# Turning a softmax tile for its second matmul: 32x32 blocks on VectorE and 2,048 transfers inside SBUF in place of 1,024 transposes on TensorE

## Chip, cores and metric

The kernel runs on one core of one Trainium2 chip. The metric is the device time of one execution in microseconds. All tensors are float32; most matmuls are made of three (below).

## What is computed

Sixteen images of 32x32 pixels with 128 channels go through two layers. The first: a depthwise 3x3 convolution with three filters per channel, two 1x1 layers with a GELU between them and a residual, then attention of each pixel over its 3x3 neighbours. The second, which the change touches, is a group norm and full attention over the 1,024 pixels of an image:

```python
xn = group_norm(x, gamma, beta)
n = H * W
xf = xn.reshape(B, n, C)
q = xf @ Wq + bq
k = xf @ Wk + bk
v = xf @ Wv + bv
attn = jnp.einsum('bnc,bmc->bnm', q, k) * scale
attn = jax.nn.softmax(attn, axis=-1)
out = jnp.einsum('bnm,bmc->bnc', attn, v)
out = out @ Wp + bp
return xn + out.reshape(B, H, W, C)
```

## The kernel before

Each engine has its program written out as calls, in an order fixed by hand-written lists: `fill_program`, then `turn_program(it)` for `it` = 1 to 12, then `drain_program`. In turn `it`, image `a = it` is in its last attention, `b = it + 1` in its local attention and group norm, `c = it + 2` in its convolution and `d = it + 3` is loaded. Engines meet through semaphores only (`Count.after(n, e)` names event `e` of image `n`). Four PSUM banks `work` are shared out by a table (`BANK_PLAN` for a turn, `FILL_PLAN` and `DRAIN_PLAN` for the ends).

A float32 product is made of three matmuls with operands split in a high part (rounded to `F32R`) and a low part (the rest): `mm3` at L468 to L470. So whoever makes an operand makes two tiles, and the low part waits for the high one.

The last attention of image `n` goes through eight tiles `t` of 128 queries:

- `scores(n, t)`, TensorE: 6 matmuls into `ps_s`, 128 queries by 1,024 keys.
- `row_max`, VectorE (L1869), then `exp`, ScalarE (L1048), from `ps_s` to the SBUF tile `e`, one tile for all `t`.
- `probs_t`, TensorE (L622): eight 128x128 transposes turn `e` so that keys lie on partitions; the result is in `ps_t`.
- `et_hi_tile`, ScalarE (L1058), copies `ps_t` to the high part; `et_lo_tile`, VectorE (L1875), subtracts to the low part. `et_hi` and `et_lo` hold four tiles each; a slot is free again when the value step of its tile pair has run.
- `values(n, j)`, TensorE: 24 matmuls for the tiles 2j and 2j+1; `a_part` (ScalarE), `attended` (TensorE) and `output` (VectorE, L1887) follow, and SyncE's `store`.

SyncE issues four x_in loads an image (`load_x`, L409; 32 partitions each) and two stores (L424). GpSimd makes the low parts of the other operands (`minus`, L1439) and the residual (`residual`, L1493 and L1496); the Winograd transform's `d` and part of `t_f` are its too. VectorE's `combine` and `combine_own` (L1737, L1744) read two operands in SBUF.

Of the kernel before, what the change touches and what calls it, by code (L numbers as in the profile page):

```python
# [31 lines left out]
F32 = mybir.dt.float32  # L32
F32R = mybir.dt.float32r
# [24 lines left out]
class Count:  # L58
# [5 lines left out]
    def after(self, n, e):  # L64
# [14 lines left out]
]  # L79
FILL_PLAN = [  # L80
    ("conv", 0, 0, 3), ("conv", 1, 0, 0), ("conv", 2, 0, 3), ("conv", 3, 0, 1), ("conv", 4, 0, 2),
    ("conv", 5, 0, 0), ("conv", 0, 1, 3), ("conv", 1, 1, 1), ("conv", 2, 1, 2), ("conv", 3, 1, 0),
# [16 lines left out]
    ("as", 0, 14, 0), ("conv", 0, 15, 1), ("as", 1, 14, 2), ("conv", 1, 15, 3), ("as", 2, 14, 2),  # L99
    ("conv", 2, 15, 0), ("at", 0, 14, 0), ("as", 3, 14, 3), ("conv", 3, 15, 2), ("conv", 4, 15, 2),  # L100
# [12 lines left out]
]  # L113

STAGE_OF = dict(xt=0, conv=1, up2=1, q=1, k=1, v=1, av=2, at=2, gn=2, qq=2, kk=2, vv=2, pv=3, pj=3, s0=3, s1=3)
STAGE_OF["as"] = 2
BANK_OF = {(u, x): bank for u, x, bank in BANK_PLAN}
FILL_BANK_OF = {(u, x, n): bank for u, x, n, bank in FILL_PLAN}
DRAIN_BANK_OF = {(u, x, n): bank for u, x, n, bank in DRAIN_PLAN}
USES = FILL_PLAN + [(u, x, it + 3 - STAGE_OF[u], bank) for it in range(1, B - 3) for u, x, bank in BANK_PLAN  # L120
                    if it + 3 - STAGE_OF[u] < B] + DRAIN_PLAN

# [13 lines left out]
def bank_number(user, x, n):  # L136

    at = n - 3 + STAGE_OF[user] if isinstance(n, int) else 1
    return FILL_BANK_OF[user, x, n] if at < 1 else DRAIN_BANK_OF[user, x, n] if at >= B - 3 else BANK_OF[user, x]


def previous_user(user, x, n):

    m = n if isinstance(n, int) else 5 + 3 - STAGE_OF[user]
    bank = bank_number(user, x, m)
    before = USES[:USES.index((user, x, m, bank))]
    found = [(u, y, k) for u, y, k, b in before if b == bank]
    if not found:
        return user, -1, 0
    u, y, k = found[-1]  # L150
    return u, y, k if isinstance(n, int) else n + (k - m)


def conv_seq_kernel(nc, ins, out):
    ctx = ExitStack()
    with ctx:
# [13 lines left out]
        def placed(name, shape, offset, dt=F32):  # L170
# [71 lines left out]
        e = sb("e", [128, PIX])  # L242
        et_at = region("et_mem", 2 * TILES * HALF)
        et_hi, et_lo = (placed(f"et_{p}", [128, TILES, HALF], et_at + 4 * TILES * HALF * k, F32R)
                        for k, p in enumerate(("hi", "lo")))
        wc_f = placed("wc_f", [128, NT, 3, D], et_at)
# [22 lines left out]
        def score_tile(n, t):  # L269

            return work_all[:, 0:PIX] if is_last(n) and t % 2 else ps_s
# [8 lines left out]
            s=8, t=8).items()}  # L280
# [23 lines left out]
        max1_ready, e_ready, et_hi_ready, et_lo_ready = (  # L304
            count("max1_ready", 8), count("e_ready", 8), count("et_hi_ready", 8), count("et_lo_ready", 8))
# [18 lines left out]
                        vv=vv_lo_ready, pv=a_ready, pj=o_ready, s0=e_ready, s1=e_ready)  # L324
# [78 lines left out]
        def _(sp):  # L403
# [21 lines left out]

            def load_x(n):
# [4 lines left out]
            def fill_program():  # L431
# [3 lines left out]
                store(0, 0)  # L435
                load_x(4)
                store(0, 1)

            def turn_program(it):
                a, d = it, it + 3  # L440
                store(a, 0)
                if has_next(d + 1):
                    load_x(d + 1)
                store(a, 1)

            def drain_program():
                store(B - 3, 0)
                store(B - 3, 1)
                store(B - 2, 0)
                store(B - 2, 1)  # L450
# [1801 lines left out]
```

## Time and profile before

| | us |
|---|---|
| median of 3 runs (1060.2 to 1060.88) | 1060.43 |
| profiled execution, its own time | 1062.82 |
| its span, first to last instruction | 1060.8 |
| TensorE busy | 1021.0 |
| VectorE busy | 791.3 |
| ScalarE busy | 723.6 |
| GpSimd busy | 394.7 |
| mean granted TensorE clock | 0.993 |

The span is what the trace covers; the profiled execution's own time has what lies around it. Busy times are unions of an engine's instructions, and a busy TensorE can still be one whose matmuls overlap; what a step costs there is read from the start of one step to the start of the next. L numbers are lines of the kernel before.

### The profile page before, as it was taken

To read this page: it belongs to the slowest core of one execution; us is meant where nothing else is said; L and a number is where in the kernel's file an instruction comes from. 1 tells how busy PE (TensorE), PEld (TensorE's weight loads), DVE (VectorE), ACT (ScalarE), POOL (GpSimd) and SP (SyncE) were. 2 spreads that over 40 slices of the span, in tenths; PEclk is the share of its full clock that TensorE was granted. 3 is DMA by queue.
4 is the path that set the end of the run, shared out by engine and by line. 5 is a ranking of instruction groups with operands and counts; after the bars stand their busy time and mean duration, and the time that the engine had idled before them with its cause. 6 is when DMAs were issued, how large, how long until landed. Compare 5 with 4: busy or idle time off the path is not lost.

```text
span 1060.8 us, 21242 instructions
## 1 busy us (share of the span) xinstructions
PE 1021.0 (96%) x7060; PEld 939.6 (89%) x7060; DVE 791.3 (75%) x1628; ACT 723.6 (68%) x1377; POOL 394.7 (37%) x365
## 2 busy tenths in 40 slices
PE   5978999999999999999999999999999999999897
PEld 5857989999998999999899999989999898998776
DVE  6957779777877877788687777868777786777674
ACT  2566767767677776767767776776767677677463
POOL 4635252352515235251523525153351515232031
PEclk9989999999999999999999999999999999999999
DMA  5101010010201001010100101010020100000000
GB/s 91 22 1 21 1 31 11 11 32 1 40 0 30 10 10 30 0 36 4 30 10 0 40 0 30 10 30 10 0 40 0 30 10 10 11 2 11 11 21 21
DMA packets 85493, 18.64 MB, mean 18 GB/s; under 512 B 67536, under 2 KB 85328, under 8 KB 85456
## 3 DMA queue, kind: packets, MB, share of 16 engines
q1 hardware_dynamic: 84608, 17.77, 8.6%
q10 hardware_dynamic: 848, 0.39, 0.2%
q8 instruction: 22, 0.36, 0.2%
q14 instruction: 15, 0.12, 0.0%
HBM read 9.76 MB, written 8.39 MB: 17 GB/s over the span
## 4 chain that ended last, share of the span: by engine, by line
PE 89%; DVE 4%; issue 3%; ACT 2%; POOL 2%; DMA 0%; ACTq 0%; DVEq 0%; POOLq 0%
PE work L468 16%; PE work L470 15%; PE work L469 15%; PE ps_t L622 10%; PE ps_s L468 5%; PE ps_s L470 5%; PE ps_s L469 5%; PE work L540 4%; PE work L561 4%; PE work L596 2%; PE work L527 2%; PE work L549 1%; PE work L586 1%; POOL g_lo L1439 1%; DVE et_lo L1875 1%
## 5 line engine op out<-in xcount | busy, mean ns | idle before, releaser
L1869 DVE TENSOR_REDUCE nm<-ps_s 128x1 f32<-128x1024 f32 x124 | 151.5, 1222 | 78.8 <-PE ps_s L470 75.9
L1439 POOL TENSOR_TENSOR g_lo<-u,g_hi 128x512 fp32r<-128x512 f32 x60 | 78.3, 1306 | 351.0 <-ACT g_hi L969 351.0
L1058 ACT ACTIVATE et_hi<-ps_t 128x1024 fp32r<-128x1024 f32 x128 | 131.2, 1025 | 99.1 <-PE ps_t L622 99.0
L468 PE MATMUL work<-t_lo,wc_hi 128*128 128x256 f32 x576 | 170.3, 296 | 5.9 <-DVE wc_lo L1688 4.4
L1875 DVE TENSOR_TENSOR et_lo<-ps_t,et_hi 128x1024 fp32r<-128x1024 f32 x128 | 156.1, 1219 | 22.6 <-ACT et_hi L1058 21.0
L470 PE MATMUL work<-t_hi,wc_hi 128*128 128x256 f32 x576 | 162.7, 283 | 0.0
L469 PE MATMUL work<-t_hi,wc_lo 128*128 128x256 f32 x576 | 162.1, 281 | 0.0
L1048 ACT ACTIVATE e<-ps_s,nm 128x1024 f32<-128x1024 f32 x124 | 138.2, 1114 | 25.2 <-DVE nm L1869 23.4
L468 PE MATMUL work<-et_lo,vv_hi 128*128 128x256 f32 x512 | 148.6, 290 | 4.6 <-DVE r_tok L1887 3.8
L470 PE MATMUL work<-et_hi,vv_hi 128*128 128x256 f32 x512 | 145.0, 283 | 0.0
L469 PE MATMUL work<-et_hi,vv_lo 128*128 128x256 f32 x512 | 144.7, 283 | 0.0
L622 PE MATMUL ps_t<-const,e 128*128 128x128 f32 x1024 | 133.0, 273 | 4.1 <-DVE et_lo L1875 4.0
L622 PEld LDWEIGHTS ps_t<-const,e 128*128 128x128 f32 x1024 | 117.8, 141 | 18.9 <-ACT e L1048 4.8
L468 PEld LDWEIGHTS work<-t_lo,wc_hi 128*128 128x128 f32 x576 | 109.3, 190 | 6.8 <-issue 4.8
L469 PEld LDWEIGHTS work<-t_hi,wc_lo 128*128 128x128 f32 x576 | 109.6, 190 | 0.1
L470 PEld LDWEIGHTS work<-t_hi,wc_hi 128*128 128x128 f32 x576 | 109.1, 189 | 0.0
L468 PE MATMUL ps_s<-kk_lo,qq_hi 128*128 128x512 f32 x248 | 106.4, 429 | 0.7 <-ACT e L1048 0.7
L468 PEld LDWEIGHTS work<-et_lo,vv_hi 128*128 128x128 f32 x512 | 97.3, 190 | 10.8 <-issue 9.7
L470 PE MATMUL ps_s<-kk_hi,qq_hi 128*128 128x512 f32 x248 | 98.0, 395 | 0.0
L469 PEld LDWEIGHTS work<-et_hi,vv_lo 128*128 128x128 f32 x512 | 97.1, 190 | 0.7
L469 PE MATMUL ps_s<-kk_hi,qq_lo 128*128 128x512 f32 x248 | 97.7, 394 | 0.0
L470 PEld LDWEIGHTS work<-et_hi,vv_hi 128*128 128x128 f32 x512 | 97.1, 190 | 0.0
(182 smaller groups left out, 2352.1 us busy)
## 6 DMA issues: line engine op xcount, KB each, us to landing
x_in<-in_x SPq DMA_DIRECT2D x64, 128.0 KB, 3.4
out<-r_tok SPq DMA_DIRECT2D x32, 256.0 KB, 2.3
w_up_t<-in_L_conv_w_up SPq DMA_DIRECT2D x1, 384.0 KB, 4.2
y<-in_L_conv_w_qkv SPq DMA_DIRECT2D x1, 192.0 KB, 4.9
const<-in_const ACTq DMA_DIRECT2D x1, 166.0 KB, 5.8
y<-in_L_conv_w_up ACTq DMA_DIRECT2D x1, 128.0 KB, 5.3
const<-in_const ACTq DMA_DIRECT2D x1, 64.0 KB, 3.6
bv_row<-in_L_conv_b_qkv SPq DMA_DIRECT2D x1, 64.0 KB, 2.9
```

The source lines that it names most:

```text
L468: te.matmul(dst, wh, xl, start=first, stop=False)
L469: te.matmul(dst, wl, xh, start=False, stop=False)
L470: return te.matmul(dst, wh, xh, start=False, stop=last)
L527: mm = te.matmul(bank("v", half, n)[:, t * 128:(t + 1) * 128], h[:, pix], wv0[:, :], start=True, stop=True)
L540: mm = te.matmul(dst, q_c[:, t * 128:(t + 1) * 128], kp[:, 4 * t:4 * t + 6, :].rearrange("p r w -> p (r w)"), start=True, stop=True)
L561: te.matmul(dst[:, u * 128 - before:(u + 1) * 128 + behind], v_pix[:, t, :], pt[half][:, at - before:at + 128 + behind], start=(u == 0), s ...
L622: mm = te.transpose(ps_t[:, kt * 128:(kt + 1) * 128], e[:, kt * 128:(kt + 1) * 128], ident)
L1048: act.activation(e[:, :], score_tile(n, t)[:, :], ACT.Exp, bias=nm1[:, t:t + 1], accum_out=sum1[:, t:t + 1]) \
L1058: act.activation(et_hi[:, :, (t % 4) * 128:(t % 4 + 1) * 128], ps_t[:, :].rearrange("p (k c) -> p k c", k=TILES), ACT.Copy) \
L1439: return pool.tensor_tensor(dst, full, hi, ALU.subtract)
L1869: dve.tensor_reduce(nm1[:, t:t + 1], score_tile(n, t)[:, :], AX.X, ALU.max, negate=True) \
L1875: dve.tensor_tensor(et_lo[:, :, cols_], ps_t[:, :].rearrange("p (k c) -> p k c", k=TILES), et_hi[:, :, cols_].bitcast(F32), ALU.subtract). ...
```

## The change

`probs_t`, its semaphore and its 1,024 transposes go. In their place stand `turn_e` on VectorE, which transposes `e` in 32x32 blocks, and `move` on SyncE, which carries each group of 32 partitions to where it belongs, in sixteen transfers a tile. `e` and the turned tile `turned` are double. `et_f`, the full turned tile, lies in the memory of `et_lo`. `et_hi_tile` reads `et_f` in SBUF; `et_lo_tile` moves to GpSimd and works in place. The columns of `et_hi` and `et_lo` are laid out in blocks, so that `values` reads 256 columns in runs of 32. `scores` writes to `ps_s` and `ps_t` in turn, for every image.

```diff
-        e = sb("e", [128, PIX])
+        e_both = sb("e", [128, 2, PIX])
+        turned_both = sb("turned", [128, 2, 4, TILES, 32])
...
-            return work_all[:, 0:PIX] if is_last(n) and t % 2 else ps_s
+            return ps_t if t % 2 else ps_s
...
+            def move(n, t):
+                ready, read = e_turned.after(n, t), pe["pv"].after(n, t // 2 - 2)
...
+                if t % 2 == 0:
+                    sp.wait_ge(*read)
...
+                sp.wait_ge(*ready)
+                for i in range(4):
+                    for s in range(4):
+                        sp.dma_start(et_f[32 * i:32 * (i + 1), t % 4, s].rearrange("r k q -> r (k q)"),
+                                     turned_both[32 * s:32 * (s + 1), t % 2, i].rearrange("r k q -> r (k q)")) \
+                          .then_inc(e_fetched[t % 4].handle, 16)
...
-                if not is_last(n) or t == 0:
-                    te.wait_ge(*e_ready.after(n, t - 1))
...
+                te.wait_ge(*e_ready.after(n, t - 2))
...
-            def probs_t(n, t):
...
-                for kt in range(TILES):
-                    mm = te.transpose(ps_t[:, kt * 128:(kt + 1) * 128], e[:, kt * 128:(kt + 1) * 128], ident)
...
-                             (et_hi[:, kt, cols_], et_lo[:, kt, cols_]), kt == 0, kt == TILES - 1)
+                             [x[:, two, :, kt, :].rearrange("p t s q -> p (t s) q") for x in (et_hi, et_lo)],
+                             kt == 0, kt == TILES - 1)
...
-                act.wait_ge(*pe["t"].after(n, t - 1))
+                act.wait_ge(*e_turned.after(n, t - 2))
...
+            def turn_e(n, t):
+                dve.wait_ge(*e_ready.after(n, t))
+                dve.wait_ge(*e_fetched[(t - 2) % 4].after(n, (t - 2) // 4))
+                dve.transpose(turned_both[:, t % 2].rearrange("p i k q -> p k i q"),
+                              e_both[:, t % 2].rearrange("p (k i q) -> p k i q", k=TILES, i=4)).then_inc(e_turned.handle, 1)
```

All call lists and bank tables are new. `BANK_PLAN` has a fourth number, how many images ahead of the turn a step works; a turn now ends with the third value step of its image, and the fourth is in the next turn:

```diff
-    ("as", 0, 0), ("conv", 0, 2), ("as", 1, 3), ("conv", 1, 1), ("at", 0, 0), ("conv", 2, 3), ("as", 2, 2),
+    ("at", 0, 1, 3), ("as", 2, 1, 1), ("vv", 1, 0, 2), ("pv", 3, -1, 1), ("conv", 0, 2, 3), ("as", 3, 1, 0),
```

On SyncE, the rest of a turn in the loop, before, after its first store (L423 to L456 are register work and the branch back):

```order
L427 ISA
L409 ISA
L409 DMA x_in<-in_x 32x32x32
L409 ISA
L409 DMA x_in<-in_x 32x32x32
L409 ISA
L409 DMA x_in<-in_x 32x32x32
L409 ISA
L409 DMA x_in<-in_x 32x32x32
L423 REGISTER_ALU
L424 ISA
L424 DMA out<-r_tok 128x4x128
```

And now the first half of that loop's body (L441 is `move`, L426 `store`):

```order
L441 DMA et_f<-turned 32x256 x16
L432 REGISTER_ALU
L441 DMA et_f<-turned 32x256 x16
L432 ISA
L441 DMA et_f<-turned 32x256 x16
L432 REGISTER_ALU
L441 DMA et_f<-turned 32x256 x16
L425 ISA
L426 ISA
L426 DMA out<-r_tok 128x4x128
L432 ISA
L441 DMA et_f<-turned 32x256 x16
```

Eight moves of sixteen transfers stand in a turn's queue, with a store after the fourth and the four loads and a store between the sixth and the seventh.

On GpSimd, the start of a turn in the loop, before (L1493 and L1496 are the residual, L1439 low parts):

```order
L1493 TENSOR_TENSOR r_tok<-vv_hi,vv_lo 128x512
L1496 TENSOR_TENSOR r_tok<-r_tok,bp_row 128x512
L1465 ISA
L1439 TENSOR_TENSOR g_lo<-u,g_hi 128x512
L1465 REGISTER_ALU
L1439 TENSOR_TENSOR g_lo<-u,g_hi 128x512
```

And now (L1461 is `minus`, L1467 and L1477 the transform):

```order
L1461 TENSOR_TENSOR et_lo<-et_f,et_hi 128x1024
L1508 REGISTER_ALU
L1461 TENSOR_TENSOR et_lo<-et_f,et_hi 128x1024
L1465 ISA
L1467 TENSOR_TENSOR d_53<-xp 128x256 x4
L1474 REGISTER_ALU
L1475 ISA
L1477 TENSOR_TENSOR t_f<-d_54 128x8x32
```

Eight low parts of 1,024 columns a turn are now on GpSimd, between its other work.

## Rows read from the trace of the kernel before

**Rows 1.** Windows: busy us of each engine (instructions), granted clock, DMA share, GB/s.
```profile
core 0: us, PE busy (x) PEld busy (x) DVE busy (x) ACT busy (x) POOL busy (x), PEclk, DMA share, GB/s
395.60:457.90 62.30, 62.26 (x438) 57.72 (x438) 47.47 (x101) 44.81 (x85) 24.05 (x22) 1.00 0.09 17
956.00:1005.00 49.00, 44.17 (x284) 39.49 (x282) 32.90 (x72) 30.74 (x64) 5.79 (x5) 0.97 0.04 12
```

**Rows 2.** Timeline of TensorE, start and length in us; turn 1 and a later turn.
```profile
204.71 1.03 PE L622 MATMUL ps_t<-const,e 128*128 128x128 f32 x8
205.58 0.61 PE L527 MATMUL work<-wv,h 128*128 128x128 f32 x4
...
466.63 0.28 PE L468 MATMUL work<-et_lo,vv_hi 128*128 128x256 f32 x1
...
469.51 1.05 PE L527 MATMUL work<-wv,h 128*128 128x128 f32 x8
470.40 1.06 PE L596 MATMUL work<-wv,a_c 128*128 128x128 f32 x8
...
472.17 1.04 PE L622 MATMUL ps_t<-const,e 128*128 128x128 f32 x8
472.96 0.48 PE L468 MATMUL ps_s<-kk_lo,qq_hi 128*128 128x512 f32 x1
...
474.44 0.85 PE L540 MATMUL work<-kp,q_c 128*128 128x204 f32 x4
474.98 0.42 PE L468 MATMUL work<-t_lo,wc_hi 128*128 128x256 f32 x1
```

**Rows 3.** Timeline of SyncE's queue, start and length of an issue in us.
```profile
7.74 0.43 SPq L405 DMA_DIRECT2D bv_row<-in_L_conv_b_qkv  x1
...
10.12 0.43 SPq L405 DMA_DIRECT2D r_tok<-in_L_conv_Wp  x1
12.87 0.33 SPq L409 DMA_DIRECT2D x_in<-in_x  x1
```

**Rows 4.** Tiles x_in and r_tok: ns min/median/max of an issue; two timelines of one burst.
```profile
L409 SPq DMA_DIRECT2D x_in<-in_x x64: 311/434/2404, 1.2 to 837.1; - x64
...
L424 SPq DMA_DIRECT2D out<-r_tok x32: 372/412/417, 139.9 to 1058.1; - x32
...
461.44 0.35 SPq L409 DMA_DIRECT2D x_in<-in_x  x1
...
461.44 2.72 SPq L409 DMA_DIRECT2D x_in<-in_x  x4
```

**Rows 5.** DMA issues: count, KB each, median us from issue to landing.
```profile
out<-r_tok SPq DMA_DIRECT2D x32, 256.0 KB, 2.3
```

**Rows 6.** Lines by form: busy us, mean ns of one, idle before and its releasers.
```profile
L1875 DVE TENSOR_TENSOR et_lo<-ps_t,et_hi 128x1024 fp32r<-128x1024 f32 x128 | 156.1, 1219 | 22.6 <-ACT et_hi L1058 21.0
...
L1058 ACT ACTIVATE et_hi<-ps_t 128x1024 fp32r<-128x1024 f32 x128 | 131.2, 1025 | 99.1 <-PE ps_t L622 99.0
...
L1439 POOL TENSOR_TENSOR g_lo<-u,g_hi 128x512 fp32r<-128x512 f32 x60 | 78.3, 1306 | 351.0 <-ACT g_hi L969 351.0
...
L1887 DVE SCALAR_TENSOR_TENSOR r_tok<-work,rec,r_tok 128x128 f32<-128x128 f32 x128 | 36.1, 344 | 6.1 <-PE work L596 5.0
...
L1065 ACT ACTIVATE a_c<-work 128x256 f32<-128x256 f32 x64 | 24.5, 382 | 22.9 <-PE work L470 22.9
...
L1616 DVE STREAM_TRANSPOSE xp<-x_in 128x512 f32<-128x512 f32 x30 | 19.7, 691 | 0.4 <-DMA x_in<-in_x 0.3
...
L1455 POOL TENSOR_TENSOR t_f<-d 128x256 f32<-128x256 f32 x15 | 11.1, 740 | 35.5 <-DVE d L1623 35.5
```

**Rows 7.** Tile u (ns min/median/max), and timelines of VectorE and GpSimd in the fill.
```profile
L1737 DVE SCALAR_TENSOR_TENSOR u<-u x30: 671/681/1234, 37.0 to 928.9; 128x512 f32<-128x512 f32 x30
...
52.58 3.48 DVE L1744 SCALAR_TENSOR_TENSOR u_one<-u_one 128x512 f32<-128x512 f32 x2
...
52.09 1.73 POOL L1439 TENSOR_TENSOR g_lo<-u,g_hi 128x512 fp32r<-128x512 f32 x1 [1.25 <-ACT g_hi L969]
```

More of the change, by code:

```diff
@@ L424, in store @@
                 sp.dma_start(out_view[:, bass.ds(n * TILES + 4 * k, 4), :], r_tok[:, :, :]).then_inc(stored.handle, 16)
+            def move(n, t):
+                ready, read = e_turned.after(n, t), pe["pv"].after(n, t // 2 - 2)
+                if not isinstance(n, int):
+                    ready, read = ((handle, sp.to_reg(value)) for handle, value in (ready, read))
+                if t % 2 == 0:
+                    sp.wait_ge(*read)
+                if is_first(n) and t == 0:
+                    sp.wait_ge(*g_lo_ready.after(1, 3))
+                    sp.wait_ge(*h_ready.after(1, 1))
+                sp.wait_ge(*ready)
[4 more added lines that the diff above has]
+                          .then_inc(e_fetched[t % 4].handle, 16)
             def load_x(n):
@@ L434, in fill_program @@
                 load_x(3)
-                store(0, 0)
-                load_x(4)
-                store(0, 1)
+                move(0, 0)
+                move(0, 1)
+                move(0, 2)
+                move(0, 3)
             def turn_program(it):
[L440 to L444, printed above, removed]
-            def drain_program():
+                z, a, d = it - 1, it, it + 3
+                move(z, 4)
+                move(z, 5)
+                move(z, 6)
+                move(z, 7)
+                store(z, 0)
+                move(a, 0)
+                move(a, 1)
+                load_x(d)
+                store(z, 1)
+                move(a, 2)
+                move(a, 3)
+            def drain_program():
+                move(B - 4, 4)
+                move(B - 4, 5)
+                move(B - 4, 6)
+                move(B - 4, 7)
+                store(B - 4, 0)
+                move(B - 3, 0)
+                move(B - 3, 1)
+                store(B - 4, 1)
+                move(B - 3, 2)
+                move(B - 3, 3)
+                move(B - 3, 4)
+                move(B - 3, 5)
+                move(B - 3, 6)
+                move(B - 3, 7)
                 store(B - 3, 0)
+                move(B - 2, 0)
+                move(B - 2, 1)
+                move(B - 2, 2)
+                move(B - 2, 3)
                 store(B - 3, 1)
+                move(B - 2, 4)
+                move(B - 2, 5)
+                move(B - 2, 6)
+                move(B - 2, 7)
                 store(B - 2, 0)
+                move(B - 1, 0)
+                move(B - 1, 1)
+                move(B - 1, 2)
+                move(B - 1, 3)
+                move(B - 1, 4)
+                move(B - 1, 5)
                 store(B - 2, 1)
+                move(B - 1, 6)
+                move(B - 1, 7)
                 store(B - 1, 0)
                 store(B - 1, 1)
-            fill_program()
-            turn_program(1)
-            with sp.Fori(2, B - 4) as it:
-                turn_program(it)
-            turn_program(B - 4)
-            drain_program()
+            run(sp, fill_program, turn_program, drain_program)
             sp.wait_ge(*stored.after(B - 1, 1))
@@ L755, in fill_program @@
-                q(2, 1)
-                values(0, 3)
-                scores(1, 0)
-                attended(0, 1)
-                v(2, 1)
+                scores(0, 6)
+                scores(0, 7)
+                up2(2, 1)
+                k(2, 0)
+                group_moments(1)
+                q(2, 0)
+                values(0, 1)
+                v(2, 0)
+                kk(1, 0)
+                kk(1, 1)
+                qq(1, 0)
+                v(2, 1)
+                qq(1, 1)
+                k(2, 1)
@@ L987, in k_half @@
                 act.wait_ge(*pe["k"].after(n, k))
+                act.wait_ge(*pe["as"].after(n - 1, 3))
                 if is_first(n):
@@ L1198, in fill_program @@
[L1198 removed]
+                local_scale(1, 2)
+                pt_pair(1, 1)
+                pt_pair(1, 2)
+                local_exp(1, 3)
                 et_hi_tile(0, 1)
[L1200 to L1209 removed]
@@ new lines, in turn_program @@
+                t_hi_part(c, 1)
+                take(c, 0, 1)
+                t_hi_part(c, 2)
+                local_exp(b, 3)
+                et_hi_tile(a, 0)
+                pt_pair(b, 1)
+                local_scale(b, 2)
+                local_scale(b, 3)
+                take(c, 2, 3)
+                et_hi_tile(a, 1)
+                exp(a, 4)
+                pt_pair(b, 2)
+                pt_pair(b, 3)
+                gelu(c, 0)
+                gelu(c, 1)
+                g_hi_part(c, 0)
@@ new lines, in turn_program @@
+                local_scale(c, 0)
+                exp(b, 1)
+                exp(b, 2)
+                et_hi_tile(a, 7)
+                local_exp(c, 1)
+                local_exp(c, 2)
+                t_hi_part(d, 0)
+            def drain_program():
+                pt_pair(B - 2, 0)
+                t_hi_part(B - 1, 1)
+                local_scale(B - 2, 1)
+                exp(B - 3, 3)
+                a_part(B - 4, 3)
+                vv_hi_half(B - 3, 0)
+                exp(B - 3, 4)
+                take(B - 1, 0, 1)
+                vv_hi_half(B - 3, 1)
+                et_hi_tile(B - 3, 0)
+                t_hi_part(B - 1, 2)
+                pt_pair(B - 2, 1)
@@ new lines, in turn_program @@
+                turn_e(a, 7)
+                x_turn(d, 1)
+                local_mask_max(c, 0)
+                local_mask_max(c, 1)
+                qq_lo_half(b, 1)
+                row_max(b, 0)
+                row_max(b, 1)
+                transform_even(d)
+                local_rec(c, 0)
+                turn_e(b, 0)
+                row_max(b, 2)
+                local_mask_max(c, 2)
+                row_max(b, 3)
+                turn_e(b, 1)
+            def drain_program():
+                transform_two(B - 1)
+                halo_turn(B - 2, 0)
+                local_rec(B - 2, 1)
+                row_max(B - 3, 4)
+                vv_lo_half(B - 3, 0)
+                turn_e(B - 3, 2)
+                output(B - 4, 1)
+                transform_ends(B - 1)
+                halo_turn(B - 2, 1)
+                local_mask_max(B - 2, 3)
+                local_rec(B - 2, 2)
+                vv_lo_half(B - 3, 1)
+                sum_and_difference(B - 1, 1, 2, 1)
+                turn_e(B - 3, 3)
+                row_max(B - 3, 5)
```

1101 lines of the change are left out of this document (505 added, 596 removed), and 58 rows, old and new, of tables (BANK_PLAN, DRAIN_PLAN, FILL_PLAN).

## Prediction, made before the change was run

> **What bounds the kernel now.** I read the busy time by stretches first, then neighbouring instructions in one turn of the loop, then the two engines that get the new work. In a steady turn TensorE is busy 62.26 of 62.30 us, beside 47.47 on VectorE, 44.81 on ScalarE and 24.05 on GpSimd [rows 1]. So a turn is bound by TensorE's own work and by no wait. What one step costs there is the distance from its first matmul to the first of the next step: eight transposes of e start at 472.17 and the next step at 472.96, 0.79 us; those at 204.71 are followed at 205.58, 0.87 us [rows 2]. A value step of 24 matmuls runs from 466.63 to 469.51, 2.88 us [rows 2]. The lengths printed per matmul overlap and can't be summed. SyncE has 4 loads and 2 stores a turn and is idle for the rest.
>
> **The change, part by part.** (a) *TensorE loses 1,024 transposes.* Eight groups a turn at 0.79 to 0.87 us, 0.85 taken, are 6.8 us. A turn of 62.3 becomes 55.5 if nothing else ends later. In the twelve turns (image 1 to 12 as `a`) that is 82 us.
>
> (b) *SyncE gets 16 transfers a tile, 2,048 in all*, each of 32 partitions by 1 KB, issued one after another. Call the time from one issue to the next P. No such transfer is in the trace. Six loads of 128 partitions with one run each, issued back to back, start at 7.74 to 10.12: 0.43 us each and 0.475 apart, so some 0.04 lie between two issues [rows 3]. An x_in load has 32 partitions, as the new transfers have; the first of a burst took 0.33 and 0.35, the shortest of all 0.311 [rows 3, 4]. Four in a burst took 2.72 [rows 4], but each stands behind a load of 1,024 short rows, which the new transfers don't have. Bounds for P are thus 0.353 (0.311 + 0.042) and 0.475. Both ends of the new transfers lie in SBUF, so less is possible too, and a queue that costs nothing is the outer bound. I take **P = 0.39** (0.35 + 0.04): in partitions the x_in row is the nearest. A turn's queue time is 128 P, the four loads at 2.7 us and two stores at 0.41 [rows 4], with 1.4 us for register instructions and gaps (an estimate: the burst of 2.72 has four issues of at least 0.35, and part of the rest is registers): 128 P + 4.9 = 54.8 us. That is 0.7 below TensorE's 55.5. Two queues so near each other, coupled by two e buffers, two turned buffers and four et slots, will not both run without gaps; I add 1.0. **A turn is 56.5 us.**
>
> (c) *What stands behind a move.* `move(n,t)` waits for the turned tile and, at even t, for the value step that frees two slots; SyncE's loads and stores queue behind it. From the last issue of a pair to its freed slots: landing 2.3 [rows 5], the high part 1.03 [rows 6], the low part 2.4 (below), value step 2.88, together 8.6 us. With 32 P = 12.5 for the pair's own issues that is 21.1 us, and the ring of four slots gives the time of two pairs, 28. Some 7 us are left for queueing, so the slots alone do not bound.
>
> (d) *VectorE*: the low part, 1,219 ns x128, goes; a transpose of 128x1024 comes. One of 128x512 took 691 ns [rows 6], so 1.38 at most; another instruction of 1,024 columns took the 1.22. 1.25 taken, 0.2 us more a turn. Cover: 47.7 of 56.5. (e) *ScalarE* reads SBUF where it read PSUM; 1,025 ns [rows 6] kept; 10% more would be 0.8 us a turn, under a cover of 11. (f) *GpSimd* takes the low part: 512 columns took 1,306 and 256 took 740 [rows 6], so 1,024 take 2.4 us, 19 a turn: 43.3 of 56.5, covered. With that cover gone the slots would be freed late, and SyncE would wait. (g) Scores alternate between two PSUM tiles; that removes waits that cost nothing now.
>
> (h) *The ends.* Before, turn 1 begins on TensorE at 204.7 [rows 2]. The new fill has no transposes (-6.8); a value step (2.88), half a projection and half of v's transposes (0.45 each, by eight such matmuls from 469.51 to 470.40) leave it, two scores (1.48 each, 472.96 to 474.44) and two local scores (0.54 each, to 474.98) enter [rows 2]: it ends at 198. The old drain, from 204.7 + 12 x 62.3 = 952, took 109. In the new one the queue shows. At the end of turn 12 the slots allow SyncE to be in the first tile of image 13: 23.5 tiles are left, 376 P = 147 us. Stores in between are 3 us. After the last issue: landing 2.3, high 1.03, low 2.4, value step 2.88, then 0.38, 0.45 and 4 x 0.34 to the output [rows 2, 6], its landing 2.3, and some 4 of queueing: 17.
>
> **Sum:** 198 + 12 x 56.5 + 147 + 20 = 1043 us of span. The profiled run stood 2.0 above its span and 2.4 above the median of the runs shown (1062.82 against 1060.43), so the median is **1042 us**, 1.7% less. Per 0.01 us of P the time moves by 4 us in the drain, and by 19 in all once the queue bounds the turn; it meets the old time at P = 0.41.
>
> Of the issue the Trainium skill says, on its page "DMA: Bandwidth & Descriptors", under "Issuing engines are not separate DMA queues", that the sequencer's time to start a DMA is usually small beside the DMA. The trace does not agree for this size: 0.43 us to issue [rows 3] against 2.3 us until a store eight times as large has landed [rows 5]. By that rule alone the time would be that of the cheap queue below. The same page, under "Rules for kernel authors", says to coalesce many small transfers, those under 64 KB being mostly overhead; these have 32 KB, and by that rule it would be the dear queue. No run here shows a 32 KB transfer between SBUF and SBUF.
>
> **The rivals.** *The dear queue* (slower). If a transfer with one run per partition costs what the back-to-back loads did, P = 0.475, SyncE needs 65.7 us a turn, more than the old 62.3, and 179 in the drain: 198 + 788 + 179 + 20 = 1185. It decides from P = 0.41. For it: the only back-to-back rows of one run per partition [rows 3]. Against it: the shortest issue is 311 ns with 32 partitions and 372 with the 128 of a store [rows 4]. The idle that it leaves on TensorE could also lower the granted clock: it was 0.97 where TensorE was busy 44.17 of 49 us [rows 1], so part of that ran at the lower level, 1.2 GHz.
>
> *The cheap queue* (faster). At P = 0.311 to 0.353 TensorE bounds the turn, 56; the drain takes 117 to 133: 1007 to 1023, 1015 taken. A queue at no cost would leave a drain of 109 less 24 groups of transposes, 88, and a time near 955.
>
> *The port.* VectorE instructions with two SBUF inputs, ten a turn, sometimes took longer while GpSimd ran: 681 ns at the median and 1,234 at most, and 1.74 each in the two at 52.58, beside a GpSimd subtraction that took 1.73 in place of 1.31 [rows 6, 7]. GpSimd's busy share goes from 39% of a turn to 77%. If each of the ten were held by 1.1 us, VectorE would need 58.7 us a turn, and with the same 1 us of gaps the sum rises by 12 x 3.2 = 38, to 1080; it decides from some 8 us of holds a turn, and less vanishes in the cover. For it: the rows; against it: the median.
> The Trainium skill states such a hold, on its page "SBUF — State Buffer", under "Who interferes with whom": a VectorE instruction with two SBUF inputs and a GpSimd one that reads SBUF exclude each other for a whole instruction. The trace agrees at 52.58 [rows 7].
>
> *Not what it says*: the value step now reads runs of 32 columns. If that made it 0.6 times longer, 1.7 us x 4 a turn would give back all of (a), and with the drain the time is 1125. No row bears on it.
>
> **Chances.** Forecast (1026 to 1064) 0.42; dear queue 0.33; cheap queue 0.15; port 0.07; runs 0.03. Some 2.1 us, 0.2%, is about what a measurement can tell from no change here. Faster: 0.38 of the forecast's and the cheap queue, 0.53; within 0.2%: 0.05, from the forecast's upper end and the port; slower: 0.42. Eight in ten need the forecast's own range, the cheap queue and half of the dear one: 985 to 1140.
>
> **What would show it.** Start to start of the new issues on SyncE near 0.39 (0.475: dear; 0.35 or less: cheap). TensorE in a steady turn busy 55 of 56 to 57 us, its few waits ending on the low part; in the dear case SyncE has no gap and TensorE waits some 10 us a turn for the low part. A drain of 160 to 170 us with TensorE half idle. VectorE's ten instructions at 0.7 us, or at 1.2 and more with the port. The value step at 2.88. I am wrong if the turn lies under 55 or over 59, or if the drain stays near 109.

## Result, and the profile after

The changed kernel took **1494.26 us** (median; 1492.87 to 1495.01) against 1060.66 for the kernel before on the same chip: a ratio of 1.408, 95% interval 1.4056 to 1.4104. It is 41% slower. 1042 was forecast, with a range up to 1140.

The profiled execution has a span of 1493.2 us. From its page, the busy time of the engines, and the first line of the chain that ended last:

```profile
PE 1075.0 (72%) x6036; PEld 950.9 (64%) x6036; DVE 893.6 (60%) x1628; ACT 757.4 (51%) x1405; POOL 700.9 (47%) x493
...
SPq 85%; issue 9%; PE 3%; DVE 2%; ACT 1%; POOL 0%; DMA 0%; DVEq 0%; ACTq 0%
```

No compute engine is full. 85% of the chain is SyncE's queue. A steady turn, from one image's loads to the next's, in the columns of [rows 1]:

```profile
core 0: us, PE busy (x) PEld busy (x) DVE busy (x) ACT busy (x) POOL busy (x), PEclk, DMA share, GB/s
473.02:559.10 86.08, 64.33 (x368) 57.31 (x367) 54.98 (x100) 46.80 (x87) 43.27 (x30) 0.86 0.25 60
```

62.30 us have become 86.08. TensorE is busy for 64.33 of them, with 70 matmul rows fewer than in [rows 1]: it now runs part of the turn at the lower clock level, 1.2 GHz (0.86 in the mean). What SyncE does meanwhile, from the timeline of its queue (start, length of the run of issues):

```profile
499.68 38.55 SPq L441 DMA_DIRECT2D et_f<-turned  x59
538.51 0.41 SPq L426 DMA_DIRECT2D out<-r_tok  x1
539.13 20.21 SPq L441 DMA_DIRECT2D et_f<-turned  x32
559.64 2.48 SPq L411 DMA_DIRECT2D x_in<-in_x  x4
562.38 0.41 SPq L426 DMA_DIRECT2D out<-r_tok  x1
```

There is no gap of more than some 0.3 us. The 32 issues of two tiles take 20.21 us; less the last one's own 0.59, that is 19.62 over 31 distances, **0.633 us from issue to issue**. The four loads take 2.48 us and the store 0.41, much as before [rows 4]. The tile et_f (ns min/median/max), and who waited for whom:

```profile
L441 SPq DMA_DIRECT2D et_f<-turned x2048: 507/591/1707, 104.4 to 1477.1; - x187
L1074 ACT ACTIVATE et_hi<-et_f x128: 1042/1057/1074, 120.1 to 1479.0; 128x1024 fp32r<-128x1024 f32 x128
L1461 POOL TENSOR_TENSOR et_lo<-et_f,et_hi x128: 2335/2366/2866, 123.5 to 1480.1; 128x1024 fp32r<-128x1024 f32 x128
...
  ACT et_hi L1074: 405.4, 103
  DVE turned L1949: 255.9, 69
...
DMA to landing us min/median/max: 1.8/1.9/3.4
```

An issue costs 591 ns at the median, against 311 for the shortest load of [rows 4] and 430 for the rows from which the upper bound came [rows 3]. ScalarE waited 405 us for the landing and VectorE 256 us for a free buffer: the engines stand behind the queue. The estimates for the compute steps, from [rows 6], held: 1.06 us for the copy, 2.37 for GpSimd's low part, and 1,242 ns for VectorE's transpose where 1.25 us were taken.

One more row matters later. Of VectorE's two-input instructions, the transform's:

```profile
L1706 DVE SCALAR_TENSOR_TENSOR t_f<-d x30: 624/1680/2732, 15.0 to 1231.5; 128x256 f32<-128x256 f32 x30
```

In [rows 7] the tile u showed 681 ns at the median with a few near 1,234. In the kernel before, this instruction of t_f took 637 ns at the median; here the median itself is 1,680.

### The profile page after: what moved, and what is told of

The parts are those of the page before. It is cut to its first block, busy times and chain, and to the rows that moved or that the text cites. A ratio compares the mean times of both kernels' runs of the same rounds, so it can differ in the third digit from the quotient of the medians.

```text
span 1493.2 us, 21726 instructions
## 1 busy us (share of the span) xinstructions
PE 1075.0 (72%) x6036; PEld 950.9 (64%) x6036; DVE 893.6 (60%) x1628; ACT 757.4 (51%) x1405; POOL 700.9 (47%) x493
## 4 chain that ended last, share of the span: by engine, by line
SPq 85%; issue 9%; PE 3%; DVE 2%; ACT 1%; POOL 0%; DMA 0%; DVEq 0%; ACTq 0%
SPq L441 81%; SPq L411 2%; SPq L426 1%; PE ps_t L691 0%; PE work L529 0%; PE work L531 0%; PE work L530 0%; DMA wperc<-in_L_conv_w_perc 0%; PE ps_s L691 0%; PE work L622 0%; ACT p L1017 0%; SPq L432 0%; ACT L1017 0%; POOL g_lo L1461 0%; POOL et_lo L1461 0%
## 5 line engine op out<-in xcount | busy, mean ns | idle before, releaser
L1461 POOL TENSOR_TENSOR et_lo<-et_f,et_hi 128x1024 fp32r<-128x1024 f32 x128 | 304.2, 2377 | 459.6 <-ACT et_hi L1074 459.6
L1949 DVE STREAM_TRANSPOSE turned<-e 128x1024 f32<-128x1024 f32 x128 | 158.9, 1242 | 324.5 <-DMA et_f<-turned 255.9
L1074 ACT ACTIVATE et_hi<-et_f 128x1024 fp32r<-128x1024 f32 x128 | 135.2, 1056 | 405.4 <-DMA et_f<-turned 405.4
L529 PE MATMUL work<-et_lo,vv_hi 128*128 128x256 f32 x512 | 187.7, 367 | 153.6 <-POOL et_lo L1461 152.2
L529 PE MATMUL ps_s<-kk_lo,qq_hi 128*128 128x512 f32 x128 | 61.1, 477 | 69.0 <-ACT e L1069 65.3
L1461 POOL TENSOR_TENSOR t_lo<-t_f,t_hi 128x512 fp32r<-128x512 f32 x48 | 65.9, 1373 | 76.2 <-ACT t_hi L961 76.2
L1943 DVE TENSOR_REDUCE nm<-ps_s 128x1 f32<-128x1024 f32 x64 | 78.0, 1218 | 27.6 <-PE ps_s L531 27.1
L1069 ACT ACTIVATE e<-ps_s,nm 128x1024 f32<-128x1024 f32 x64 | 71.0, 1109 | 46.4 <-DVE nm L1943 41.3
L1026 ACT ACTIVATE pn<-p,rec 128x192 f32<-128x192 f32 x128 | 51.1, 448 | 79.7 <-DVE pt L1878 62.0
L1943 DVE TENSOR_REDUCE nm<-ps_t 128x1 f32<-128x1024 f32 x64 | 78.0, 1218 | 21.9 <-PE ps_t L531 21.6
L1461 POOL TENSOR_TENSOR g_lo<-u,g_hi 128x512 fp32r<-128x512 f32 x60 | 77.1, 1297 | 20.2 <-ACT g_hi L987 20.1
```

Source lines behind the costliest of these rows:

```text
L529: te.matmul(dst, wh, xl, start=first, stop=False)
L1026: ins_ = act.activation(pn[:, u, :].rearrange("p (r w) -> p r w", r=6), p0[:, 2 * (j % 2) + u, :, 1:1 + W], ACT.Copy, scale=rec0[:, t:t + 1])
L1069: act.activation(e_both[:, t % 2], score_tile(n, t)[:, :], ACT.Exp, bias=nm1[:, t:t + 1], accum_out=sum1[:, t:t + 1]) \
L1074: act.activation(et_hi[:, t % 4].rearrange("p s k q -> p (s k q)"), et_f[:, t % 4].rearrange("p s k q -> p (s k q)"), ACT.Copy).then_inc(e ...
L1461: return pool.tensor_tensor(dst, full, hi, ALU.subtract)
L1943: dve.tensor_reduce(nm1[:, t:t + 1], score_tile(n, t)[:, :], AX.X, ALU.max, negate=True) \
```

## Experiments

Line numbers are those of each kernel; an inserted or deleted line shifts them by a few. The two kernels through device memory were timed four times, the others once each; no difference in time that is read below as an effect is smaller than 3%.

### What an issue costs, by shape

76 transfers were put into the fill, where SyncE idles, for example:

```diff
+                for r in range(8):
+                    sp.dma_start(ef[0:32, 256 * r:256 * r + 256], const[32:64, 0:256]).then_inc(probed.handle, 16)
...
+                for r in range(8):
+                    sp.dma_start(tf[64:96, 256 * r:256 * r + 256], ins["const"][32:64, 0:256]).then_inc(probed.handle, 16)
```

> The changed kernel with 76 more transfers early in the fill, where SyncE is idle: ten shapes, four or eight of each back to back, so that the distance from issue to issue is read for each. Theory 1 (both ends in SBUF make the issue dear): 0.63 us with 32, 64 and 128 partitions alike, and under 0.5 where one end is in device memory. Theory 2 (32 partitions make it dear, whichever memory): 0.6 for 32 partitions from device memory too, 0.475 for 128 partitions. Theory 3 (bytes): the 32 by 256 B transfer costs under 0.45, the 128 by 1 KB over 1. The time of the kernel itself is that of the change, 1494.

The timeline of SyncE's queue in that stretch (eight issues a row, four of kk_hi); `scratch` and `in_const` lie in device memory, the other tiles in SBUF:

```profile
30.38 6.38 SPq L460 DMA_DIRECT2D e<-const  x8
36.81 5.03 SPq L462 DMA_DIRECT2D e<-const  x8
41.88 5.03 SPq L464 DMA_DIRECT2D e<-const  x8
46.96 5.46 SPq L466 DMA_DIRECT2D e<-const  x8
52.46 5.06 SPq L468 DMA_DIRECT2D turned<-const  x8
57.57 3.83 SPq L470 DMA_DIRECT2D turned<-in_const  x8
61.45 2.42 SPq L472 DMA_DIRECT2D kk_hi<-const  x4
63.92 5.38 SPq L474 DMA_DIRECT2D kk_lo<-const  x8
69.33 3.85 SPq L476 DMA_DIRECT2D scratch<-const  x8
73.22 5.01 SPq L478 DMA_DIRECT2D scratch<-in_const  x8
```

In order: 32 partitions by 1 KB across partitions (the change's own shape), the same without crossing, 32 by 256 B, 16 by 1 KB, 64 by 1 KB, a load of 32 by 1 KB, 128 by 1 KB, 128 by 512 B, a store of 32 by 1 KB, and device memory to device memory. Wherever both ends lie inside SBUF, eight take 5.03 to 5.06 us, 0.63 from issue to issue (6.38, 5.46 and 5.38 hold one late issue each). Partitions and bytes do not matter for these shapes, which all have one run per partition: 8 KB and 128 KB cost the same. Where one end is in device memory, eight take 3.83 to 3.85, 0.46 from issue to issue, also with 32 partitions. With both ends in device memory it is 0.63 again. So theory 1 holds, in a wider form: both ends in the same kind of memory are dear, which no theory had said of device memory. Theories 2 and 3 fall.

### A second queue

The eight kk_lo transfers were moved to ScalarE, four while SyncE issues and four while it is idle.

```diff
                 t_hi_part(1, 0)
+                act.wait_ge(*const_loaded.after(0, 0))
+                for r in range(4):
+                    act.dma_start(kk_lo[:, 128 * r:128 * r + 128].bitcast(F32), const[:, 0:128]).then_inc(probed_act.handle, 16)
```

> The probe of the fill again, with eight of its transfers inside SBUF issued by ScalarE: four while SyncE issues its own back to back, four while SyncE is idle. Theory 1 (each engine pays for its own issues): 0.63 us on both queues at both times. Theory 2 (one unit serves both): while both issue, the distance from issue to issue rises to about 1.2 us on both, and falls back to 0.63 on ScalarE alone. By theory 2 a second queue would not have helped the change. The time of the kernel is that of the change.

ScalarE's two bursts, from the timeline of its queue:

```profile
35.63 2.67 ACTq L1178 DMA_DIRECT2D kk_lo<-const  x4
...
85.17 2.43 ACTq L1221 DMA_DIRECT2D kk_lo<-const  x4
```

And SyncE's issues beside the first of them, in the same kernel:

```profile
36.06 5.11 SPq L462 DMA_DIRECT2D e<-const  x8
```

5.11 us against 5.03 alone, and 2.67 against 2.43: each engine pays for its own issues. Theory 1 holds.

### Fewer issues for the same bytes

Half the issues and one issue a tile, both with wrong blocks in the turned tile; and a whole computation with five issues, the turned tile going through device memory:

```diff
-                    for s in range(4):
+                    for s in range(0, 4, 2):
-                        sp.dma_start(et_f[32 * i:32 * (i + 1), t % 4, s].rearrange("r k q -> r (k q)"),
-                                     turned_both[32 * s:32 * (s + 1), t % 2, i].rearrange("r k q -> r (k q)")) \
+                        sp.dma_start(et_f[32 * i:32 * (i + 1), t % 4, s:s + 2].rearrange("r s k q -> r (s k q)"),
+                                     turned_both[32 * s:32 * (s + 1), t % 2, s:s + 2].rearrange("r i k q -> r (i k q)")) \
```

> Eight transfers a tile of 32 partitions by 2 KB in place of sixteen by 1 KB: the same bytes into the same tile, half the issues, the wrong blocks (the products of the last attention are not those of the reference). Theory (the queue: 0.633 us from one issue to the next whatever its bytes, so that 128 of them set the turn of 86.08): SyncE needs 64 x 0.633 + 4.9 = 45.4 us a turn, TensorE is the bound again at 55.5 to 57, and the time falls to 1000 to 1040. Rival 1 (the issue is paid by bytes): 1.2 us an issue, turn 86 and time 1494 as with the change. Rival 2 (VectorE and GpSimd hold each other at the SBUF port, and the queue only waits): the issues are fewer but the turn stays above 65, time above 1150.

```diff
+                sp.dma_start(et_f[:, t % 4].rearrange("p s k q -> p (s k q)"),
+                             turned_both[:, t % 2].rearrange("p i k q -> p (i k q)")) \
```

> One transfer a tile of 128 partitions by 4 KB, without moving anything between partitions: the same bytes, one issue, wrong blocks (the products of the last attention are not those of the reference). It shows the change with next to no queue. Theory (the queue): SyncE needs under 12 us a turn; the turn is TensorE's 55.5 to 57 and the drain 90 to 105 us, together 955 to 990. Rival 2 (the port): VectorE's two-input instructions stay at 1.2 to 1.6 us and the turn is above 60, time above 1030. Rival 3 (reading 32-column runs made the value step longer than 2.88 us): turn above 59 with TensorE full, time above 1010.

```diff
+                for s in range(4):
+                    sp.dma_start(bounce[t % 2, :, :, s].rearrange("i r x -> r i x"),
+                                 turned_both[32 * s:32 * (s + 1), t % 2].rearrange("r i k q -> r i (k q)")) \
+                      .then_inc(bounced.handle, 16)
+                sp.wait_ge(*there)
+                sp.dma_start(et_f[:, t % 4].rearrange("p s k q -> p (s k q)"),
+                             bounce[t % 2].rearrange("i r s x -> (i r) (s x)")) \
+                  .then_inc(e_fetched[t % 4].handle, 16)
```

> The whole computation, with the turned tile carried through device memory: four stores of 32 partitions and one load of 128 partitions a tile, 5 issues where there were 16; SyncE waits for the stores' landing before it issues the load. Theory (the queue): 8 tiles x (4 x 0.6 + some 2.6 for the landing + 0.5) + 4.9 = 49 us of queue a turn, less than TensorE's 55.5, so a time of 980 to 1030, faster than both kernels. Rival 1 (bytes): each store of 128 KB costs what four of 32 KB did, 2.5 us, 8 x 13 + 5 = 109 us a turn and a time above 1600. Rival 2 (the port): above 1100.

Measured: 1128.71, 1117.96 and 1127.28 us (the last a ratio of 1.0613, interval 1.0598 to 1.0628). A steady turn of each, by windows in the same columns as above, first with half the issues:

```profile
480.00:544.60 64.60, 57.59 (x371) 51.32 (x371) 53.96 (x101) 45.37 (x86) 42.96 (x30) 0.97 0.35 81
```

with one:

```profile
488.76:553.36 64.60, 58.68 (x376) 52.14 (x375) 55.93 (x100) 46.35 (x88) 43.35 (x31) 0.97 0.26 81
```

through device memory:

```profile
482.00:546.60 64.60, 58.60 (x376) 52.04 (x375) 55.97 (x101) 46.34 (x88) 43.38 (x31) 0.97 0.56 146
```

Two things follow. The queue is what separates 1494 us from some 1120: at 64 issues a turn, each still 591 ns at the median, the turn falls by 21.5 us, and from 64 to 8 it falls no further. The rival that the issue is paid by bytes falls. But the theory's other number, 55.5 to 57 us a turn, fell too, and all three times missed its ranges; the rival of the port had two of them right (above 1030 and above 1100). **At 64.6 stands a second floor**, above the old 62.3, that has nothing to do with the number of issues: without the queue the change would still have been slower.

### What holds the turn at 64.6

In the kernel with one transfer no engine is full: TensorE 58.7, VectorE 55.9, ScalarE 46.4, GpSimd 43.4 of 64.6. Its timeline of GpSimd shows t_lo and the residual:

```profile
495.32 1.56 POOL L1459 TENSOR_TENSOR t_lo<-t_f,t_hi 128x512 fp32r<-128x512 f32 x1
496.82 1.55 POOL L1518 TENSOR_TENSOR r_tok<-vv_hi,vv_lo 128x512 f32<-128x512 f32 x1
498.45 1.41 POOL L1521 TENSOR_TENSOR r_tok<-r_tok,bp_row 128x512 f32<-128x512 f32 x1
```

and that of VectorE, at the same time, two pairs of the transform's instructions with two SBUF inputs:

```profile
494.70 2.68 DVE L1704 SCALAR_TENSOR_TENSOR t_f<-d 128x256 f32<-128x256 f32 x2
497.20 3.16 DVE L1713 SCALAR_TENSOR_TENSOR t_f<-d 128x256 f32<-128x256 f32 x2
```

5.7 us for four that take 2.6 in the kernel before (637 and 676 ns at the median). VectorE's time in a turn goes from 47.47 us [rows 1] to 55.93. The four t_f (1,414 and 1,664 ns at the median) make 3.5 of these 8.5 us. Another 2.8 lie in three instructions of the group norm that have one column each and two inputs in SBUF, which the prediction did not count; one of them, 150 ns at the median in the kernel before:

```profile
L1910 DVE TENSOR_TENSOR gn<-cols,gn x16: 159/1239/1249, 91.0 to 1045.2; 128x1 f32<-128x1 f32 x16
```

And TensorE's waits, here the longest sum (the next is 25.3 us for g_lo, another low part of GpSimd's):

```profile
PE work L527 <- POOL et_lo L1459: 30.9, 16, 4.5
```

Two candidates, then: VectorE's instructions held while GpSimd works, and GpSimd's low part coming late; the third is the call orders. The holds were cut by reading one input:

```diff
-                    ins_ = dve.scalar_tensor_tensor(t_f[:, k, :, 1:1 + W], d[:, 1], two, d[:, 2], ALU.mult, ALU.add)
+                    ins_ = dve.tensor_scalar(t_f[:, k, :, 1:1 + W], d[:, 1], two, 0.0, ALU.mult, ALU.add)
...
-                dve.tensor_tensor(gn_a, gamma, rstd, ALU.mult).then_inc(gn_step.handle, 1)
+                dve.tensor_scalar(gn_a, gamma, 1.0, 0.0, ALU.mult, ALU.add).then_inc(gn_step.handle, 1)
```

> The kernel with one transfer a tile (turn 64.6 with next to no queue), in which VectorE's ten large instructions with two SBUF inputs a turn (d, t_f, u) and four small ones (moments, gn) read one input only; GpSimd keeps its eight low parts a turn. Left out are the second operands of those instructions, so the convolution's and the norm's values are not those of the reference. Theory (the hold: these instructions wait while GpSimd reads SBUF, 8.4 us a turn of VectorE's 55.9, and what TensorE waits for comes late): the turn falls to 56 to 59 and the time to 990 to 1030. Rival 1 (GpSimd's low part itself comes late, 1.05 us of exp's copy and 2.4 us a tile, before the value step): the turn stays at 62 to 65, the time at 1080 to 1118. Rival 2 (the new call orders chain the engines so, whatever these two do): the same 62 to 65.

the low part by cutting it to 32 columns, with the value step taking the high part in its place:

```diff
-                minus(et_lo[:, t % 4].rearrange("p s k q -> p (s k q)"), et_f[:, t % 4].rearrange("p s k q -> p (s k q)"),
-                      et_hi[:, t % 4].rearrange("p s k q -> p (s k q)").bitcast(F32)).then_inc(et_lo_ready.handle, 1)
+                minus(et_lo[:, t % 4, 0, 0], et_f[:, t % 4, 0, 0], et_hi[:, t % 4, 0, 0].bitcast(F32)).then_inc(et_lo_ready.handle, 1)
```

> The kernel with one transfer a tile, in which GpSimd's low part covers 32 columns in place of 1,024, and the value step takes the high part in place of the low one: GpSimd is freed of 8 x 2.3 us a turn, and with it most of the holds. Left out is the low part of the exponentials. Theory (the hold) and rival 1 (the late low part): both give a turn of 55 to 58 and 970 to 1020; the VectorE instructions go back to 0.7 us. Rival 2 (the call orders): the turn stays at 62 or more. With the other run of this call: both fall, the hold; only this one, the late low part; neither, the orders.

and both:

> One transfer a tile, GpSimd's low part cut to 32 columns, and VectorE's large instructions with two SBUF inputs reading one: the two cuts of the runs before in one kernel. Left out are the low part of the exponentials and the second operands. If the holds and the late low part together are what keeps the turn at 64.6 (theory 1), they add: 55.5 to 58 us a turn, a time of 960 to 1010. If the rest is the new call orders, a chain through the engines that comes round once a turn (theory 2), the turn stays at 59.5 to 61.5 as in the kernel with one input, 1040 to 1060.

Measured: 1059.59, 1079.13 and 1025.34 us. A turn with one input:

```profile
474.00:535.10 61.10, 56.83 (x376) 51.17 (x377) 51.44 (x101) 46.81 (x89) 43.42 (x31) 1.00 0.28 86
```

with the short low part:

```profile
470.00:532.60 62.60, 57.26 (x370) 51.17 (x369) 51.21 (x97) 46.36 (x87) 25.23 (x29) 0.97 0.26 79
```

with both:

```profile
467.10:526.10 59.00, 56.39 (x376) 50.86 (x375) 47.94 (x101) 46.39 (x88) 26.09 (x30) 1.00 0.28 89
```

64.6 falls by 3.5, by 2.0 and by 5.6: the two cuts add, and neither alone reaches what the theory of the holds expected (56 to 59 and 55 to 58). No single theory has all three: with one input the turn lies between the two bands, with the short low part it lies in the band of the call orders (62 or more), and with both it lies between again. TensorE's waits tell what each cut took away. With one input those for et_lo stay (30.6 us, 30.9 without the cut) and those for VectorE's vv_lo fall from 15.5 to 3.0. With the short low part those for et_lo fall to 4.8, and those for vv_lo rise to 30.3. So both candidates are real, and behind each the other stands close. The first edit also makes the instructions themselves shorter (t_f at its shortest 395 ns, 622 before it), so the 3.5 are not holds alone. Nor did it free them all: a one-input instruction that it did not touch was now held, the group norm's (544 ns at the median in the kernel before), from the tile y:

```profile
L1912 DVE TENSOR_SCALAR y<-y,gn x32: 533/1134/1487, 87.0 to 990.0; 128x512 f32<-128x512 f32 x32
```

The Trainium skill names this on its page "SBUF — State Buffer", under "Who interferes with whom": besides instructions with two SBUF inputs, tensor_scalar in a mode that uses both ports can contend with GpSimd. The trace agrees, with 1,134 ns at the median where 544 are enough; which mode the instruction ran in no run shows.

The kernel with the short low part shows one thing more. GpSimd is busy 25.23 us of its turn, hardly more than the 24.05 of [rows 1], and yet VectorE's 51.21 are 3.7 above the old 47.47: two of its t_f still take 1,690 ns at the median, and the instruction of the group norm above 1,236. So part of the holds comes with the new call orders, which put these instructions beside GpSimd's, and not with GpSimd's added work.

### The same two questions in the old orders

Two of the eight transposes a tile, in the kernel before:

```diff
-                for kt in range(TILES):
+                for kt in (6, 7):
```

> The kernel before with two of the eight transposes a tile: TensorE loses six of eight, some 0.64 us a tile and 5.1 a turn, in the old call orders; nothing else changes. Left out are six eighths of the transposed exponentials. If a turn is bound by TensorE's own work alone, as the prediction has it (theory 1): 62.3 - 5.1 = 57.2 us a turn and a time of 975 to 995. If another chain of waits stands close behind TensorE (theory 2): the turn stays at 60 to 62 and the time at 1030 to 1058.

Eight subtractions more on GpSimd, in the kernel before, spread over the turn:

```diff
+            def dummy(n, i):
+                pool.wait_ge(*dummied.after(n - 1, i - 1))
+                minus(pad[:, 2 * PIX:3 * PIX], pad[:, 0:PIX], pad[:, PIX:2 * PIX]).then_inc(dummied.handle, 1)
```

> The kernel before, whole, with eight more subtractions of 128 x 1,024 a turn on GpSimd that nobody reads, as many as the change's low parts there. Theory 1 (the hold costs VectorE some 8 us a turn wherever GpSimd is busy, but VectorE has 15 us of cover in the old orders): VectorE's busy time in a turn goes from 47.5 to 52 to 57, and the time from 1060 to 1060 to 1085. Theory 2 (GpSimd's own results come late behind the added work, or the held VectorE instructions stand in a chain without slack): above 1100.

Measured: 1003.89 and 1127.04 us. A turn with fewer transposes:

```profile
451.50:509.90 58.40, 57.76 (x392) 52.09 (x391) 46.84 (x101) 44.97 (x85) 24.03 (x23) 1.00 0.09 18
```

TensorE stays full to within 0.7 us, so the premise that TensorE bounds the old turn holds, though the turn and the time lie a little above what was expected. TensorE's busy time fell by 4.5 us for 48 transposes, 0.094 each, and the turn by 3.9, since 0.6 became waiting. The 64 that the change removes are worth 6.0 us of TensorE's time by that, not 6.8.

And with more work on GpSimd:

```profile
480.00:547.40 67.40, 64.11 (x449) 58.71 (x448) 52.54 (x102) 45.84 (x88) 43.92 (x31) 1.00 0.08 17
```

This stretch is a little more than one turn (449 matmuls where a turn has 438): the turns take 66.4 to 67.9 us. **Eight instructions that nobody waits for cost some 5 us a turn** in a kernel whose GpSimd was busy 39% of it. From the tile t_f of that kernel, its median 637 ns in the kernel before:

```profile
L1649 DVE SCALAR_TENSOR_TENSOR t_f<-d x30: 616/1183/1197, 27.6 to 967.8; 128x256 f32<-128x256 f32 x30
```

and of TensorE's waits the two longest in the loop, which came to 0.4 and 2.6 us in the kernel before:

```profile
PE work L543 <- DVE vv_lo L1879: 26.4, 13, 2.2
PE work L471 <- POOL h_lo L1442: 14.8, 14, 2.1
```

VectorE is held, GpSimd's own results come late, and TensorE waits for both. Theory 2 of that run holds. In the loop it is not the added instructions that run beside VectorE's t_f but GpSimd's own d and t_f (in one turn from 494.94 to 498.98 us), which come after the added ones in its order and did not meet VectorE's in the kernel before.

### The low part back on VectorE

A whole computation once more, through device memory, with et_lo on VectorE where GpSimd had it:

```diff
-                pool.wait_ge(*et_hi_ready.after(n, t))
...
+                dve.wait_ge(*et_hi_ready.after(n, t))
```

> The whole computation through device memory (five issues a tile) with the low part back on VectorE, from SBUF, at the places where GpSimd did it. GpSimd has its 24 us a turn again, VectorE 47.7 + 8 x 1.22 = 57.5. Theory (GpSimd's added work, by the holds and by its late results, is what keeps the turn at 64.6 once the queue is gone): VectorE becomes the bound with little slack, 59 to 62.5 us a turn, a time of 1030 to 1075, below the 1127 of the kernel with the low part on GpSimd. Rival (the new orders keep the turn at 64 whichever engine makes the low part, or a full VectorE is worse than a held one): 1110 to 1160.

1200.92 us, a ratio of 1.1313 (interval 1.1294 to 1.1332). The theory missed; the rival had the direction, and its range up to 1160 was too low as well. A turn:

```profile
480.00:549.80 69.80, 60.33 (x376) 52.74 (x375) 62.84 (x109) 46.45 (x88) 26.42 (x23) 0.95 0.52 135
```

VectorE is busy 62.84 of 69.80, more than the old turn: 57.5 had been expected, and the holds came on top, with GpSimd busy 26.42. None of the whole computations here is faster than the kernel before.

## Why the prediction was wrong, step by step

- **(b) P, the step that failed first.** The prediction bounded P by 0.353 and 0.475 us and took 0.39 because, "in partitions the x_in row is the nearest". It measured 0.633, outside both ends, and partitions turned out not to matter at all. The rows for the bounds were loads from device memory [rows 3, 4]; what counts is that both ends lie in SBUF, which no row of before showed. The prediction did allow that "less is possible too" for that reason; it allowed nothing above 0.475. The short issues of 0.311 to 0.35 us, from which it took the lower end and the 0.39, were short for another reason than their partitions: each came after a pause of 2.3 us or more. In the kernel through device memory four equal stores show it, the first alone and then all four:

```profile
485.58 0.32 SPq L442 DMA_DIRECT2D bounce<-turned  x1
485.58 1.76 SPq L442 DMA_DIRECT2D bounce<-turned  x4
```

  The first takes 0.32 us, the other three some 0.48 each. That the one dearer row, four loads in 2.72 us [rows 4], was an effect of short rows is not contradicted: a load of 32 partitions by 1 KB was issued every 0.46 us.
- **The formula around P was right.** With 0.633 in the prediction's own sum: turn 128 x 0.633 + 4.9 = 85.9 (measured 86.08), drain 376 x 0.633 = 238, and 198 + 12 x 85.9 + 238 + 20 = 1487 us of span; 1493.2 was measured. This is the rival of the dear queue: it had the place right, its price was that of loads from device memory and a quarter too low, and it had 0.33.
- **(a) TensorE's gain** was somewhat mis-sized: 6.8 us a turn in the sum, 6.0 by the run with fewer transposes, and 5.9 by the kernel with both cuts (56.39 busy against 62.26). The distance from start to start of a group [rows 2] is more than what goes away with the group.
- **(d) and (f), "covered"**, failed, though their sums held: GpSimd's 43.35 came as reckoned, and VectorE's own new work, eight transposes at 1.24 us in place of eight low parts at 1.22, is 0.2 more. What failed is that neither was hidden. With the queue out of the way the turn was 64.6, not 56.5. Of these 8.1 us, 0.9 is (a): TensorE needs 56.39 where 55.5 were reckoned. Another 2.3 are its work at the lower clock: 58.68 busy with one transfer a tile, 56.39 with both cuts, for the same 376 matmuls, at a granted clock of 0.97 and 1.00. The other 4.9 are waits: 5.9 us, where the prediction added 1.0 for coupling.
- **The port rival** was real in its mechanism. It was to decide from some 8 us of holds a turn, and VectorE went up by 8.5 us in the kernel with one transfer. But it let the turn be set by a full VectorE, and VectorE was busy only 55.93 of 64.6: the holds cost by making others wait. Its price of 1080 lies 38 us under that kernel's 1118, and its chance was 0.07. "Against it: the median" [rows 7] argued from a kernel in which GpSimd was busy 39% of the time, and from the one tile, u, whose median hardly moved (679 ns with the change).
- **A queue at no cost** was priced at 955. One issue a tile took 1118. So the cheap queue was no way to a gain either, and the break-even at P = 0.41 did not exist: two separate errors, each of which alone turns the sign.
- (c), (e) and (g) are not contradicted: the copy took 1.06 us, and landing 1.9 against 2.3 assumed. **Runs of 32 columns** cost nothing that shows: in the kernel with one transfer a value matmul at full clock follows the last by 0.12 us (the timeline at the end of this document), 24 of them 2.9 us, as in [rows 2].
- What stays open: with both cuts the turn is 59.0 us, 2.6 above TensorE's 56.39. TensorE's two longest waits there are for g_lo and vv_lo, 1.5 and 0.8 us a time:

```profile
PE work L527 <- POOL g_lo L1459: 22.1, 15, 1.8
PE work L599 <- DVE vv_lo L1928: 9.3, 12, 0.9
```

  Whether the call orders or the remaining holds make these two late was not taken apart.

## What to carry to other kernels

Before work is moved to a queue in thousands of small transfers, find the price of an issue of exactly that kind (which memory at either end, back to back, not the first after a pause); if no row shows it, its upper bound is open, and a probe of eight transfers in an idle stretch settles it. Bytes were free here and issues were not: go for fewer and larger transfers, or share them over two engines' queues. And a busy share far below the turn is no cover: eight more instructions on a GpSimd busy 39% cost some 5 us of 62, by delaying what stands behind them in GpSimd's own order and so by holding VectorE. What decides is not the share but which instructions the order puts side by side; short ones count too, where others wait for them.

## What the runs showed that was not expected

- Issue to issue, with one run per partition and whatever the size: 0.63 us inside SBUF and inside device memory, 0.46 between the two. The way through device memory issues its four stores in 1.76 us, where sixteen direct transfers take some 10. The Trainium skill's page "DMA: Bandwidth & Descriptors", under "Issuing engines are not separate DMA queues", has it that issuing on several engines at once saves the sequencers' time alone; here that time was the bound (0.633 of issue in a row, against 1.9 us to land, with several in flight), and two queues paid theirs side by side.
- After a wait TensorE lost more at the lower clock. In the kernel with one transfer it waits 1.88 us for a low part until 495.59; the value step that follows begins at full clock and then runs at half of it, 1.2 GHz, although nothing is missing any more. From TensorE's timeline:

```profile
495.59 0.39 PE L527 MATMUL work<-et_lo,vv_hi 128*128 128x256 f32 x1 [1.88 <-POOL et_lo L1459]
...
496.31 0.29 PE L529 MATMUL work<-et_hi,vv_hi 128*128 128x256 f32 x1
496.43 0.28 PE L527 MATMUL work<-et_lo,vv_hi 128*128 128x256 f32 x1
...
497.04 0.42 PE L528 MATMUL work<-et_hi,vv_lo 128*128 128x256 f32 x1
```

and by windows (PEclk is the number after the five engines):

```profile
495.59:496.83 1.24, 1.24 (x10) 1.24 (x10) 1.24 (x2) 1.00 (x3) 1.24 (x2) 0.96 0.79 284
496.83:500.03 3.20, 3.20 (x17) 3.20 (x16) 3.20 (x3) 0.00 (x0) 2.96 (x3) 0.50 1.26 188
```

The matmuls stand 0.12 us apart at first and then 0.21; fifteen of them, from 496.83 to 500.03, lose 1.4 us on top of the 1.88. In the kernel with both cuts this wait is gone from the loop, and the granted clock is 1.00 in the mean of the turn.
